# Householder tridiagonalization: sums over partitions in four column groups, and dot products formed by TensorE in the last 127 steps

## The chip, the cores and the metric

One NeuronCore of a Trainium2 chip runs the whole program. The metric is the device time in microseconds of one execution. TensorE is PE in the rows below (PEld its weight loads), VectorE DVE, ScalarE ACT, GpSimd POOL and SyncE SP.

## What is computed

The reference runs a graph network with LSTM windows on `x` (16 x 512 x 128) and `adj` (512 x 512), adds it to `x`, normalizes, then runs a spectral graph network and normalizes again. The spectral network needs all eigenvectors `U` of a symmetric 512 x 512 matrix:

```python
deg = jnp.sum(A, axis=0) + jnp.sum(A, axis=1) - jnp.diagonal(A)
d_inv_sqrt = jnp.where(deg > 0, jax.lax.rsqrt(deg), 0.0)
L_norm = d_inv_sqrt[:, None] * (jnp.diag(deg) - A) * d_inv_sqrt[None, :]
_, U = jnp.linalg.eigh(L_norm)
h = jax.nn.relu(jnp.einsum('mn,bnd->bmd', U.T, features) @ W1 + b1)
return jnp.einsum('nm,bmd->bnd', U, h @ W2 + b2)
```

The kernel finds them by reducing `L_norm` to tridiagonal form with Householder reflectors, solving that small problem, and turning the vectors back. Everything is float32. The change lies in the reduction.

## The kernel before

The matrix stands in SBUF as `lap`, 128 partitions x 4 tiles x 512 columns. The reduction is one loop of 510 steps (`STEPS`), written out in full on each engine; the engines meet through semaphores. Step k works on column k + 1 below the diagonal, in the tiles from `t0 = (k + 1) // 128` on, so on T = 4 - t0 tiles: T is 4 for the first 127 steps, 3 and 2 for 128 each, 1 for the last 127. Updates of the matrix are held back in a panel of 16 steps (`NB`, `j = k % 16`); the panel is the last 128 columns of `lapw`. Every 16th step PE applies it as a rank-32 product (L581 to L586), and DVE adds that to `lap` (L990).

In a step, with `a` the column (`acols[:, t0:, k]`), `v` the reflector, and `y`, `p`, `w` vectors of the same length:

- DVE's `norms` (L969, L970) puts the head of `a` (alpha) and each partition's share of a.a into `xn`. PE sums over the partitions with a matmul whose weights are all ones (L574); the total then stands in every partition of PSUM bank 0. ACT takes the root (L349), and DVE forms the reflector from it (L994 to L1004).
- PE forms the product of the matrix and panel with `a` (L591): the weights are the column `a`, repeated in 32 columns, and four column groups of the array each stream their own strips of 32 columns of each tile. For this loop there are 8 T matmuls in the trace, since each float32 matmul stands there as two.
- PE picks the row of the panel that the reflector starts in (L595, a 128-column weight `unit(k)`), and sums the squares of the tail (L599), which POOL has prepared (L307 to L320).
- DVE reduces the products to `ycol` and `a1` (L1007 to L1021), multiplies and reduces v.y to one number a partition (L1023), PE sums it (L601); the same for v.p (L1041, L603). The sum of v.y is needed for the next column (L1044), that of v.p for `w` (L1049, L1052).
- L1044 writes column k + 1 of `acols`; `norms(k + 1)` follows at once, then L1049 and L1052, then the next step's L994. L1052 releases the next step's L591.

All five partition sums and the panel row are a 128 x 128 weight and one or a few moving columns:

```python
pe.matmul(bank[0][:, 0:2], ones[:, 0:P], xn[:, 0:2], start=True, stop=True).then_inc(norm_ps, 1)
pe.matmul(bank[3][:, 0:1], ones[:, 0:P], xp[:, 0:1], start=True, stop=True).then_inc(vy_ps, 1)
```

The order of work on each engine is the order in which it stands in the code; nothing else schedules it. PE takes for step k: L574, L591, L595, L599, L601, L603. DVE's order is its list above; `put` and `after` are semaphores between DVE's own instructions. ACT takes in a step L349, L352 (copy of `w`), L358, L360 and L361 (copies of `v`), L363 (`w0`, p times tau) and L365. POOL takes L307 and one to four more for the tail.

Of the kernel before, what the change touches and what calls it, by code (L numbers as in the profile page):

```python
# [5 lines left out]
ALU = mybir.AluOpType  # L6
ACT = mybir.ActivationFunctionType
# [5 lines left out]
P = 128  # L13
N = 512
# [132 lines left out]
def program(nc, x, adj, wg0, bg0, wg1, bg1, wih, whh, bih, bhh, w1, b1, w2, b2, out):  # L147
    with ExitStack() as ctx:
        def sb(name, shape, dt=F32):
            return ctx.enter_context(nc.sbuf_tensor(name, shape, dt))  # L150

        def sem(name):
            return ctx.enter_context(nc.semaphore(name))
# [13 lines left out]
        a1 = sb("a1", [P, NT]); ycol = sb("ycol", [P, NT]); pcol = sb("pcol", [P, NT])  # L167
        bm = sb("bm", [P, NT]); ats = sb("ats", [P, NT]); w0 = sb("w0", [P, NT]); jcol = sb("jcol", [P, 3, NT]); xp = sb("xp", [P, 2]); ts = sb("ts", [P, 8])
        tail = sb("tail", [P, N])
# [65 lines left out]
        a_ready = sem("a_ready"); norm_in = sem("norm_in"); tail_link = sem("tail_link"); tail_in = sem("tail_in"); tail_ps = sem("tail_ps"); v2_ready = sem("v2_ready"); edge_ready = sem("edge_ready"); p_ready = sem("p_ready"); w0_ready = sem("w0_ready"); norm_ps = sem("norm_ps"); norm_root = sem("norm_root"); rowz_ps = sem("rowz_ps")  # L235
        y_done = sem("y_done"); x_ready = sem("x_ready"); vy_ps = sem("vy_ps"); vy_saved = sem("vy_saved"); x2_ready = sem("x2_ready"); vp_ps = sem("vp_ps")
        w_ready = sem("w_ready"); w2_ready = sem("w2_ready"); panx_ps = sem("panx_ps"); panx_sb = sem("panx_sb"); update_ps = sem("update_ps"); updated = sem("updated")
# [40 lines left out]
        def _(pool):  # L278
# [53 lines left out]
        def _(act):  # L332
# [204 lines left out]
        def _(pe):  # L537
# [29 lines left out]
            def unit(k):  # L567
                return ident[:, (k + 1) % P:(k + 1) % P + 1].to_broadcast([P, P])

            for k in range(STEPS):  # L570
                t0, j = (k + 1) // P, k % NB
                T, c0 = NT - t0, t0 * P
                pe.wait_ge(norm_in, 2 * (k + 1))
                pe.matmul(bank[0][:, 0:2], ones[:, 0:P], xn[:, 0:2], start=True, stop=True).then_inc(norm_ps, 1)  # L574
                if k:
# [23 lines left out]
                pe.matmul(bank[4][:, 0:1], ones[:, 0:P], xn[:, 2:3], start=True, stop=True).then_inc(tail_ps, 1)  # L599
                pe.wait_ge(x_ready, k + 1)  # L600
                pe.matmul(bank[3][:, 0:1], ones[:, 0:P], xp[:, 0:1], start=True, stop=True).then_inc(vy_ps, 1)  # L601
                pe.wait_ge(x2_ready, k + 1)
                pe.matmul(bank[2][:, 4 * NB:4 * NB + 1], ones[:, 0:P], xp[:, 1:2], start=True, stop=True).then_inc(vp_ps, 1)  # L603
# [269 lines left out]
        def _(dve):  # L873
# [108 lines left out]
            for k in range(STEPS):  # L982
                t0, j = (k + 1) // P, k % NB
                T, c0 = NT - t0, t0 * P
                v, a_ = vcols[:, t0:, k], acols[:, t0:, k]
                if j == 0 and k:
                    for t in range(t0, NT):
                        adds += 1
                        dve.wait_ge(update_ps, adds)
                        m = V.tensor_tensor(lap[:, t, first_live(k):], lap[:, t, first_live(k):], bank[4 + t][:, first_live(k):], ALU.add)  # L990
                    m.then_inc(updated, 1)

                dve.wait_ge(norm_root, k + 1)
                put(V.reciprocal(ts[:, 3:4], ts[:, 0:1]))  # L994
                a = put(V.tensor_scalar(ts[:, 1:2], bank[0][:, 1:2], 0.0, 0.5, ALU.is_ge, ALU.subtract))
# [4 lines left out]
                b = put(V.scalar_tensor_tensor(pair[:, k, 1:2], ts[:, 4:5], ts[:, 1:2], bank[0][:, 1:2], ALU.mult, ALU.add))  # L1000
                after(a)
# [14 lines left out]
                after(a)  # L1016
                y = put(V.tensor_reduce(ycol[:, t0:], yz[:, t0:, 0:32 + 2 * j], AX.X, ALU.add))  # L1017
# [11 lines left out]
                p = put(V.scalar_tensor_tensor(pcol[:, t0:], a1[:, t0:], pair[:, k, 0:1], ycol[:, t0:], ALU.mult, ALU.add))  # L1029
                after(g)  # L1030
# [9 lines left out]
                c = put(V.scalar_tensor_tensor(ats[:, t0:], a_, scrow[:, k:k + 1], ltm[:, t0:, k + 1], ALU.mult, ALU.mult))  # L1040
                V.tensor_tensor_reduce(jcol[:, 2, t0:], v, pcol[:, t0:], 0.5, 0.0, ALU.mult, ALU.add, xp[:, 1:2]).then_inc(x2_ready, 1)  # L1041
# [9 lines left out]
                dve.wait_ge(w0_ready, k + 1)  # L1051
                V.scalar_tensor_tensor(pan[:, t0:, :, j, 0], v.unsqueeze(2).to_broadcast([P, T, 4]), ts[:, 6:7], w0[:, t0:].unsqueeze(2).to_broadcast([P, T, 4]),  # L1052
# [911 lines left out]
```

## Time and profile before

| | |
|---|---|
| time, median of 3 runs | 5219.31 us (5218.76 to 5219.66) |
| time of the profiled execution | 5220.33 us |
| its span | 5218.5 us |
| DVE busy | 4171.1 us, 80% |
| PE busy | 3302.7 us, 63% |
| chain that ended last | DVE 61%, PE 30%, issue 6%, ACT 1% |
| reduction (first L994 to the last) | 56.4 to 2756.4 us |

The profile is one execution. The chain that ended last goes backwards from the end, at each step to what released the waiting instruction. A row's idle time is that of its engine just before it, with what ended it. Ends of matmuls are modelled. What follows the reduction is the LSTM network, the tridiagonal solver and the spectral network; the change leaves their instructions as they are.

### The profile page before, as it was taken

Reading aid. Unit: us, or ns where it says so; the run is one execution under the profiler, and the core shown is the slowest. Engines: PE = TensorE matmul, PEld = TensorE weight load, DVE = VectorE, ACT = ScalarE, POOL = GpSimd, SP = SyncE. Lnnn points to the kernel's source line nnn. Section 1 sums busy time; section 2 is a strip of 40 time slices with the busy share of each in tenths; the row PEclk is TensorE's granted clock in tenths of the full one; section 3 lists DMA queues with packets and bytes.
Section 4 is the critical chain, followed back from the end, with each engine's and each line's share of the span. In section 5 each row is a group of like instructions: output and inputs, shape, how many; then the busy total and the mean of one; then the engine's idle time right before and its main releaser. Section 6 shows DMA issues by size and latency. Waiting matters only on the chain.

```text
span 5218.5 us, 76031 instructions
## 1 busy us (share of the span) xinstructions
PE 3302.7 (63%) x18918; PEld 2330.4 (45%) x18918; DVE 4171.1 (80%) x26705; ACT 1070.2 (21%) x4761; POOL 362.2 (7%) x1807
## 2 busy tenths in 40 slices
PE   6888888878887777777776764656722232234148
PEld 4556665666666666666663221222212232223124
DVE  7666666777777888888888999999977888988956
ACT  1111111222222222222221123433301200200001
POOL 1111111111111111100000000000000000000000
PEclk5555555555555555555557777878955555656669
DMA  2000000000000000000000000000000000000001
GB/s 65 1 1 1 1 1 1 2 1 1 2 1 1 1 1 1 1 1 1 1 1 1 1 1 1 1 1 1 1 1 1 0 0 0 0 0 0 0 0 33
DMA packets 20810, 17.51 MB, mean 3 GB/s; under 512 B 6544, under 2 KB 16784, under 8 KB 20368
## 3 DMA queue, kind: packets, MB, share of 16 engines
q1 hardware_dynamic: 20368, 12.65, 0.9%
q8 instruction: 152, 2.49, 0.2%
q14 instruction: 290, 2.38, 0.2%
HBM read 8.41 MB, written 4.20 MB: 2 GB/s over the span
## 4 chain that ended last, share of the span: by engine, by line
DVE 61%; PE 30%; issue 6%; ACT 1%; SPq 0%; DMA 0%; POOL 0%; DVEq 0%
PE bank L591 10%; PE bank L603 6%; PE bank L595 3%; PE bank L574 3%; DVE qp L1384 2%; DVE ycol L1017 2%; DVE dif L1746 2%; PE bank L586 2%; DVE tau_row L1033 2%; DVE ts L1049 2%; DVE qp L1371 2%; DVE jcol L1041 2%; DVE gated L1031 1%; DVE lapw L1052 1%; DVE pcol L1029 1%
## 5 line engine op out<-in xcount | busy, mean ns | idle before, releaser
L591 PE MATMUL bank<-lapw,hid 128*32 128x160 f32 (+3 forms) x10200 | 660.4, 421 | 59.1 <-DVE lapw L990 16.2
L662 PE MATMUL bank<-hid,rows 128*128 128x512 f32 (+1 forms) x504 | 318.2, 797 | 275.8 <-ACT dif L397 273.6
L591 PEld LDWEIGHTS bank<-lapw,hid 128*32 128x32 f32 x10200 | 394.7, 162 | 184.2 <-DVE lapw L1052 82.2
L603 PE MATMUL bank<-xp,ones 128*128 128x1 f32 x1020 | 298.9, 362 | 278.6 <-DVE xp L1041 278.6
L601 PE MATMUL bank<-xp,ones 128*128 128x1 f32 x1020 | 298.9, 362 | 185.4 <-DVE xp L1023 185.4
L603 PEld LDWEIGHTS bank<-xp,ones 128*128 128x128 f32 x1020 | 255.3, 311 | 322.1 <-DVE xp L1041 322.1
L601 PEld LDWEIGHTS bank<-xp,ones 128*128 128x128 f32 x1020 | 255.3, 311 | 229.1 <-DVE xp L1023 229.1
L360 ACT ACTIVATE swap<-vcols 128x4 f32<-128x4 f32 (+3 forms) x510 | 105.5, 207 | 1148.6 <-DVE xp L1023 1148.6
L662 PEld LDWEIGHTS bank<-hid,rows 128*128 128x128 f32 x504 | 117.1, 239 | 468.4 <-ACT dif L397 299.6
L574 PE MATMUL bank<-xn,ones 128*128 128x2 f32 x1020 | 299.2, 363 | 18.6 <-DVE xn L970 17.3
L595 PEld LDWEIGHTS bank<-lapw,ident 128*128 128x128 f32 x956 | 240.2, 313 | 157.9 <-issue 157.9
L595 PE MATMUL bank<-lapw,ident 128*128 128x2 f32 (+1 forms) x956 | 291.9, 385 | 0.0
L599 PE MATMUL bank<-xn,ones 128*128 128x1 f32 x1020 | 289.1, 353 | 0.0
L599 PEld LDWEIGHTS bank<-xn,ones 128*128 128x128 f32 x1020 | 277.5, 332 | 10.6 <-issue 10.6
L1007 DVE TENSOR_TENSOR yz<-bank,pick 128x128 f32<-128x128 f32 (+3 forms) x510 | 117.8, 231 | 204.2 <-PE bank L591 204.0
L574 PEld LDWEIGHTS bank<-xn,ones 128*128 128x128 f32 x1020 | 255.3, 311 | 44.5 <-DVE xn L970 20.9
L307 POOL TENSOR_TENSOR sq<-hid,ltm 128x4 f32<-128x4 f32 (+3 forms) x510 | 101.0, 198 | 2302.3 <-DVE hid L1044 2250.6
L745 PE MATMUL bank<-wide,ones 128*128 128x128 f32 x80 | 18.3, 402 | 293.1 <-DVE wide L1502 293.1
L1049 DVE TENSOR_SCALAR ts<-bank,tau_row 128x1 f32<-128x1 f32 x510 | 141.4, 277 | 64.4 <-PE bank L603 1.1
L349 ACT ACTIVATE ts<-bank 128x1 f32<-128x1 f32 x510 | 87.2, 171 | 456.2 <-PE bank L574 456.2
L363 ACT ACTIVATE w<-pcol,tau_row 128x4 f32<-128x4 f32 (+3 forms) x510 | 150.9, 296 | 115.0 <-DVE tau_row L1033 115.0
L994 DVE RECIPROCAL ts<-ts 128x1 f32<-128x1 f32 x510 | 83.3, 163 | 101.1 <-ACT ts L349 100.8
(752 smaller groups left out, 7994.1 us busy)
## 6 DMA issues: line engine op xcount, KB each, us to landing
out_x<-xs SPq DMA_DIRECT2D x16, 256.0 KB, 3.0
lapw<-in_adj SPq DMA_DIRECT2D x1, 1024.0 KB, 5.6
bias_rows<-in_L_gnn_bg SPq DMA_DIRECT2D x8, 64.0 KB, 6.0
hid<-pair SPq DMA_DIRECT2D x32, 1.0 KB, 1.7
bias_rows<-in_L_gnn_b SPq DMA_DIRECT2D x4, 64.0 KB, 5.8
wg<-in_L_gnn_Wg SPq DMA_DIRECT2D x2, 64.0 KB, 4.9
wg<-in_L_gnn_W SPq DMA_DIRECT2D x2, 64.0 KB, 4.5
dif<-in_L_gnn_Wih SPq DMA_DIRECT2D x1, 0.5 KB, 6.4
```

What stands on the lines that cost most here:

```text
L360: act.activation(swap[:, t0:, j, 0], vcols[:, t0:, k], ACT.Copy)
L363: act.activation(w0[:, t0:], pcol[:, t0:], ACT.Copy, scale=tau_row[:, k:k + 1]).then_inc(w0_ready, 1)
L574: pe.matmul(bank[0][:, 0:2], ones[:, 0:P], xn[:, 0:2], start=True, stop=True).then_inc(norm_ps, 1)
L586: pe.matmul(bank[4 + t][:, first_live(k):], panx[:, 0, t * P:(t + 1) * P], panx[:, 1, first_live(k):], start=True, stop=True).then_inc(upd ...
L591: m = pe.matmul(bank[1][32 * q:32 * q + 32, 0:(T + 1) * 32].rearrange("p (u i) -> p u i", i=32), acols[:, t, k:k + 1].to_broadcast([P, 32] ...
L595: pe.matmul(bank[2][:, 0:2 * j], unit(k), lapw[:, t0, N:N + 2 * j], start=True, stop=True).then_inc(rowz_ps, 1)
L599: pe.matmul(bank[4][:, 0:1], ones[:, 0:P], xn[:, 2:3], start=True, stop=True).then_inc(tail_ps, 1)
L601: pe.matmul(bank[3][:, 0:1], ones[:, 0:P], xp[:, 0:1], start=True, stop=True).then_inc(vy_ps, 1)
L603: pe.matmul(bank[2][:, 4 * NB:4 * NB + 1], ones[:, 0:P], xp[:, 1:2], start=True, stop=True).then_inc(vp_ps, 1)
L662: m = pe.matmul(bank[4 * h + q][:, 0:cols_], wih_t[:, p - 1, q * P:(q + 1) * P], hid[:, b0:b0 + nb, t:t + (nw - 1) * p + 1:p], start=True, ...
L1007: a = put(V.tensor_tensor(yz[:, t0:, 0:32], bank[1][:, 0:T * 32].rearrange("p (t i) -> p t i", i=32), pick[:].unsqueeze(1).to_broadcast([P ...
L1049: a = put(V.tensor_scalar(ts[:, 6:7], bank[2][:, 4 * NB:4 * NB + 1], tau_row[:, k:k + 1], tau_row[:, k:k + 1], ALU.mult, ALU.mult))
```

## The change

Two things change. First, `everywhere` replaces each full-width sum and the panel row by four matmuls, one for each column group, with 32 weight columns each; every group writes its own 32 partitions of the same PSUM column. This holds in all 510 steps.

Second, in the steps with one tile left (`dots(k)`, k from 383 to 509) PE forms four dot products itself with `product`: one vector is the weight, repeated in 32 columns, the other the moving column. These are a.a (alpha comes from a sum of its own with `unit(k)`), the tail, v.y and v.p. `norms`, L1023 and L1041 fall away on DVE in these steps, and POOL's second product. The small constants that those instructions carried move: 1e-32 of a.a becomes a bias `tiny` of 1e-30 under ACT's root, and the factor 0.5 of v.p becomes a copy of tau times 0.5 on ACT (`ts[:, 7:8]`). DVE's wait for `w0_ready` stands one instruction earlier in all steps.

```diff
+DOT_TILES = 1
+def dots(k):
+    return NT - (k + 1) // P <= DOT_TILES
...
 (POOL)
                 if k:
                     pool.wait_ge(tail_ps, k)
+                if dots(k):
+                    pool.tensor_tensor(sq[:, 0, t0:], acols[:, t0:, k], ltm[:, t0:, k + 1], ALU.mult).then_inc(tail_in, 1)
+                    continue
...
 (ACT)
-                act.activation(ts[:, 0:1], bank[0][:, 0:1], ACT.Sqrt).then_inc(norm_root, 1)
+                if dots(k):
+                    act.activation(ts[:, 0:1], bank[0][:, 0:1], ACT.Sqrt, bias=tiny[:]).then_inc(norm_root, 1)
+                else:
+                    act.activation(ts[:, 0:1], bank[0][:, 0:1], ACT.Sqrt).then_inc(norm_root, 1)
...
                 act.wait_ge(p_ready, k + 1)
+                if dots(k):
+                    act.activation(ts[:, 7:8], tau_row[:, k:k + 1], ACT.Copy, scale=0.5)
...
 (PE)
             def unit(k):
-                return ident[:, (k + 1) % P:(k + 1) % P + 1].to_broadcast([P, P])
+                return ident[:, (k + 1) % P:(k + 1) % P + 1].to_broadcast([P, 32])
+            def everywhere(into, weights, column):
+                for q in range(4):
+                    m = pe.matmul(into[32 * q:32 * q + 32, :], weights, column, start=True, stop=True)
+                return m
+            def product(into, left, right):
+                for q in range(4):
+                    for t in range(T):
+                        m = pe.matmul(into[32 * q:32 * q + 32, :], left[:, t:t + 1].to_broadcast([P, 32]), right[:, t:t + 1], start=(t == 0), stop=(t == T - 1))
+                return m
...
-                pe.wait_ge(norm_in, 2 * (k + 1))
-                pe.matmul(bank[0][:, 0:2], ones[:, 0:P], xn[:, 0:2], start=True, stop=True).then_inc(norm_ps, 1)
+                if dots(k):
+                    pe.wait_ge(a_ready, k + 1)
+                    product(bank[0][:, 0:1], acols[:, t0:, k], acols[:, t0:, k]).then_inc(norm_ps, 1)
+                    everywhere(bank[5][:, 0:1], unit(k), acols[:, t0, k:k + 1]).then_inc(alpha_ps, 1)
+                else:
+                    pe.wait_ge(norm_in, 2 * (k + 1))
+                    everywhere(bank[0][:, 0:2], ones[:, 0:32], xn[:, 0:2]).then_inc(norm_ps, 1)
...
-                    pe.matmul(bank[2][:, 0:2 * j], unit(k), lapw[:, t0, N:N + 2 * j], start=True, stop=True).then_inc(rowz_ps, 1)
+                    everywhere(bank[2][:, 0:2 * j], unit(k), lapw[:, t0, N:N + 2 * j]).then_inc(rowz_ps, 1)
...
+                if dots(k):
+                    product(bank[4][:, 0:1], sq[:, 0, t0:], sq[:, 0, t0:]).then_inc(tail_ps, 1)
+                    pe.wait_ge(x_ready, k + 1)
+                    product(bank[3][:, 0:1], vcols[:, t0:, k], ycol[:, t0:]).then_inc(vy_ps, 1)
+                    pe.wait_ge(x2_ready, k + 1)
+                    product(bank[2][:, 4 * NB:4 * NB + 1], vcols[:, t0:, k], pcol[:, t0:]).then_inc(vp_ps, 1)
+                else:
+                    everywhere(bank[4][:, 0:1], ones[:, 0:32], xn[:, 2:3]).then_inc(tail_ps, 1)
...
 (DVE)
+                alpha = bank[5][:, 0:1] if dots(k) else bank[0][:, 1:2]
...
                 dve.wait_ge(norm_root, k + 1)
+                if dots(k):
+                    scalars += 1
+                    dve.wait_ge(alpha_ps, scalars)
...
+                if dots(k):
+                    V.tensor_reduce(ycol[:, t0:], yz[:, t0:, 0:32 + 2 * j], AX.X, ALU.add).then_inc(x_ready, 1)
...
-                after(max(y, vdone))
-                V.tensor_tensor_reduce(jcol[:, 1, t0:], v, ycol[:, t0:], 1.0, 0.0, ALU.mult, ALU.add, xp[:, 0:1]).then_inc(x_ready, 1)
+                if not dots(k):
+                    after(max(y, vdone))
+                    V.tensor_tensor_reduce(jcol[:, 1, t0:], v, ycol[:, t0:], 1.0, 0.0, ALU.mult, ALU.add, xp[:, 0:1]).then_inc(x_ready, 1)
...
-                if k + 1 < STEPS:
+                if k + 1 < STEPS and not dots(k + 1):
                     norms(k + 1)
                 dve.wait_ge(vp_ps, k + 1)
-                a = put(V.tensor_scalar(ts[:, 6:7], bank[2][:, 4 * NB:4 * NB + 1], tau_row[:, k:k + 1], tau_row[:, k:k + 1], ALU.mult, ALU.mult))
+                dve.wait_ge(w0_ready, k + 1)
+                half = ts[:, 7:8] if dots(k) else tau_row[:, k:k + 1]
+                a = put(V.tensor_scalar(ts[:, 6:7], bank[2][:, 4 * NB:4 * NB + 1], tau_row[:, k:k + 1], half, ALU.mult, ALU.mult))
```

L1029 (`pcol`) releases `x2_ready` in these steps, and L1041 is left out in the same way as L1023.

## Rows read from the trace of the kernel before

**Rows 1.** Busy time by stretch: T = 4, 3, 2 and 1; PEclk is the clock.

```profile
56.40:898.40 842.00, 694.24 (x5438) 505.21 (x5434) 546.68 (x3822) 155.39 (x904) 125.44 (x635) 0.50 0.01 1
898.40:1609.80 711.40, 572.56 (x4436) 454.72 (x4432) 527.63 (x3849) 154.67 (x914) 100.25 (x511) 0.50 0.01 1
1609.80:2207.40 597.60, 470.85 (x3384) 386.84 (x3380) 490.98 (x3841) 150.97 (x914) 74.92 (x383) 0.50 0.01 1
2207.40:2756.40 549.00, 396.99 (x2289) 333.39 (x2288) 455.63 (x3772) 145.35 (x900) 48.60 (x252) 0.50 0.00 1
```

**Rows 2.** DVE by line: T = 4 (two rows), 3, 2; after the bar idle us.

```profile
L1007 DVE TENSOR_TENSOR yz<-bank,pick 128x128 f32<-128x128 f32 x127 | 37.1, 292 | 155.7 <-PE bank L591 155.7
L1015 DVE TENSOR_TENSOR tz<-swap,bank 128x8 f32<-128x8 f32 (+14 forms) x119 | 26.3, 221 | 11.0
...
L1015 DVE TENSOR_TENSOR tz<-swap,bank 128x90 f32<-128x90 f32 (+14 forms) x120 | 24.6, 205 | 17.0 <-PE bank L595 6.0
...
L1015 DVE TENSOR_TENSOR tz<-swap,bank 128x60 f32<-128x60 f32 (+14 forms) x120 | 22.5, 188 | 2.8
```

**Rows 3.** Timeline of one step with T = 3: start, us, instruction, idle before.

```profile
1599.82 0.87 PE L591 MATMUL bank<-lapw,hid 128*32 128x128 f32 x12
...
1600.76 0.26 DVE L1007 TENSOR_TENSOR yz<-bank,pick 128x96 f32<-128x96 f32 x1 [0.37 <-PE bank L591]
1600.93 0.23 DVE L1012 TENSOR_TENSOR yz<-swap,bank 128x78 f32<-128x78 f32 x1
...
1601.44 0.33 DVE L1017 TENSOR_REDUCE ycol<-yz 128x3 f32<-128x174 f32 x1
...
1601.90 0.09 DVE L1023 DVE_READ_ACCUMULATOR2_ANT xp<- 128x1 f32 x1
1601.90 0.16 DVE L1025 TENSOR_SCALAR vrow<-bank 128x1 f32<-128x1 f32 x1
...
1603.17 0.58 PE L603 MATMUL bank<-xp,ones 128*128 128x1 f32 x2 [0.54 <-DVE xp L1041]
...
1603.60 0.08 DVE L970 DVE_READ_ACCUMULATOR2_ANT xn<- 128x1 f32 x1
...
1603.80 0.28 DVE L1049 TENSOR_SCALAR ts<-bank,tau_row 128x1 f32<-128x1 f32 x1
```

**Rows 4.** Timeline with T = 1: one step's end, then the next step's y and a1.

```profile
2602.88 0.22 DVE L1040 SCALAR_TENSOR_TENSOR ats<-hid,scrow,ltm 128x1 f32<-128x1 f32 x1
...
2603.14 0.23 DVE L1044 SCALAR_TENSOR_TENSOR hid<-ats,bank,bm 128x1 f32<-128x1 f32 x1
...
2604.40 0.17 ACT L349 ACTIVATE ts<-bank 128x1 f32<-128x1 f32 x1 [0.83 <-PE bank L574]
...
2604.45 0.44 PE L591 MATMUL bank<-lapw,hid 128*32 128x64 f32 x8
...
2604.60 0.16 DVE L994 RECIPROCAL ts<-ts 128x1 f32<-128x1 f32 x1 [0.20 <-ACT ts L349]
...
2605.98 0.17 DVE L1021 TENSOR_REDUCE a<-tz 128x1 f32<-128x21 f32 x1
...
2606.26 0.21 DVE L1029 SCALAR_TENSOR_TENSOR pcol<-a,pair,ycol 128x1 f32<-128x1 f32 x1
```

**Rows 5.** PE matmuls by form: ns min/median/max of one, first and last start.

```profile
L591 PE MATMUL bank<-lapw,hid x8: 314/315/316, 2604.5 to 2604.6; 128*32 128x64 f32 x8
...
L591 PE MATMUL bank<-lapw,hid x24: 421/421/423, 1604.4 to 1605.5; 128*32 128x128 f32 x24
...
L603 PE MATMUL bank<-xp,ones x1020: 352/362/373, 60.5 to 2759.5; 128*128 128x1 f32 x170
...
L595 PE MATMUL bank<-lapw,ident x18: 371/394/417, 1481.4 to 1523.0; 128*128 128x14 f32 x2, 128*128 128x16 f32 x2, 128*128 128x18 f32 x2, 128*128 128x20 f32 x2
```

**Rows 6.** ACT in one step with T = 3, from the timeline.

```profile
1602.56 0.30 ACT L363 ACTIVATE w<-pcol,tau_row 128x3 f32<-128x3 f32 x1 [0.21 <-DVE tau_row L1033]
...
1604.41 0.20 ACT L352 ACTIVATE swap<-lapw 128x3 f32<-128x3 f32 x1
```

More of the change, by code:

```diff
@@ L167, in program @@
         a1 = sb("a1", [P, NT]); ycol = sb("ycol", [P, NT]); pcol = sb("pcol", [P, NT])
-        bm = sb("bm", [P, NT]); ats = sb("ats", [P, NT]); w0 = sb("w0", [P, NT]); jcol = sb("jcol", [P, 3, NT]); xp = sb("xp", [P, 2]); ts = sb("ts", [P, 8])
+        bm = sb("bm", [P, NT]); ats = sb("ats", [P, NT]); w0 = sb("w0", [P, NT]); jcol = sb("jcol", [P, 3, NT]); xp = sb("xp", [P, 2]); tiny = sb("tiny", [P, 1]); ts = sb("ts", [P, 8])
         tail = sb("tail", [P, N])
@@ L235, in program @@
         a_ready = sem("a_ready"); norm_in = sem("norm_in"); tail_link = sem("tail_link"); tail_in = sem("tail_in"); tail_ps = sem("tail_ps"); v2_ready = sem("v2_ready"); edge_ready = sem("edge_ready"); p_ready = sem("p_ready"); w0_ready = sem("w0_ready"); norm_ps = sem("norm_ps"); norm_root = sem("norm_root"); rowz_ps = sem("rowz_ps")
-        y_done = sem("y_done"); x_ready = sem("x_ready"); vy_ps = sem("vy_ps"); vy_saved = sem("vy_saved"); x2_ready = sem("x2_ready"); vp_ps = sem("vp_ps")
+        y_done = sem("y_done"); alpha_ps = sem("alpha_ps"); x_ready = sem("x_ready"); vy_ps = sem("vy_ps"); vy_saved = sem("vy_saved"); x2_ready = sem("x2_ready"); vp_ps = sem("vp_ps")
         w_ready = sem("w_ready"); w2_ready = sem("w2_ready"); panx_ps = sem("panx_ps"); panx_sb = sem("panx_sb"); update_ps = sem("update_ps"); updated = sem("updated")
@@ L598, in _ @@
                 pe.wait_ge(tail_in, k + 1)
[L599 to L603, printed above, removed]
+                if dots(k):
[6 more added lines that the diff above has]
+                    everywhere(bank[4][:, 0:1], ones[:, 0:32], xn[:, 2:3]).then_inc(tail_ps, 1)
+                    pe.wait_ge(x_ready, k + 1)
+                    everywhere(bank[3][:, 0:1], ones[:, 0:32], xp[:, 0:1]).then_inc(vy_ps, 1)
+                    pe.wait_ge(x2_ready, k + 1)
+                    everywhere(bank[2][:, 4 * NB:4 * NB + 1], ones[:, 0:32], xp[:, 1:2]).then_inc(vp_ps, 1)
             j = STEPS % NB
@@ L606, in _ @@
             pe.wait_ge(v2_ready, STEPS)
-            pe.matmul(bank[2][:, 0:2 * j], unit(STEPS), lapw[:, NT - 1, N:N + 2 * j], start=True, stop=True).then_inc(rowz_ps, 1)
+            everywhere(bank[2][:, 0:2 * j], unit(STEPS), lapw[:, NT - 1, N:N + 2 * j]).then_inc(rowz_ps, 1)
             pe.wait_ge(diag_in, 1)
@@ L946, in _ @@
             V.memset(swap[:], 0.0)
+            V.memset(tiny[:], 1e-30)
             V.memset(pair[:], 0.0)
@@ L973, in _ @@
             adds = 0
-            rowz = 0
+            rowz = scalars = 0
             def panel_rows(row, j, T):
@@ L993, in _ @@
                 dve.wait_ge(norm_root, k + 1)
+                if dots(k):
+                    scalars += 1
+                    dve.wait_ge(alpha_ps, scalars)
                 put(V.reciprocal(ts[:, 3:4], ts[:, 0:1]))
-                a = put(V.tensor_scalar(ts[:, 1:2], bank[0][:, 1:2], 0.0, 0.5, ALU.is_ge, ALU.subtract))
+                a = put(V.tensor_scalar(ts[:, 1:2], alpha, 0.0, 0.5, ALU.is_ge, ALU.subtract))
                 after(a)
@@ L999, in _ @@
                 a = put(V.tensor_tensor(pair[:, k, 0:1], ts[:, 4:5], ts[:, 1:2], ALU.mult))
-                b = put(V.scalar_tensor_tensor(pair[:, k, 1:2], ts[:, 4:5], ts[:, 1:2], bank[0][:, 1:2], ALU.mult, ALU.add))
+                b = put(V.scalar_tensor_tensor(pair[:, k, 1:2], ts[:, 4:5], ts[:, 1:2], alpha, ALU.mult, ALU.add))
                 after(a)
@@ L1016, in _ @@
                 after(a)
-                y = put(V.tensor_reduce(ycol[:, t0:], yz[:, t0:, 0:32 + 2 * j], AX.X, ALU.add))
+                if dots(k):
+                    V.tensor_reduce(ycol[:, t0:], yz[:, t0:, 0:32 + 2 * j], AX.X, ALU.add).then_inc(x_ready, 1)
+                else:
+                    y = put(V.tensor_reduce(ycol[:, t0:], yz[:, t0:, 0:32 + 2 * j], AX.X, ALU.add))
                 if j:
@@ L1028, in _ @@
                     dve.wait_ge(w0_ready, k)
-                p = put(V.scalar_tensor_tensor(pcol[:, t0:], a1[:, t0:], pair[:, k, 0:1], ycol[:, t0:], ALU.mult, ALU.add))
+                p = V.scalar_tensor_tensor(pcol[:, t0:], a1[:, t0:], pair[:, k, 0:1], ycol[:, t0:], ALU.mult, ALU.add)
+                if dots(k):
+                    p.then_inc(x2_ready, 1)
+                else:
+                    put(p)
                 after(g)
@@ L1040, in _ @@
                 c = put(V.scalar_tensor_tensor(ats[:, t0:], a_, scrow[:, k:k + 1], ltm[:, t0:, k + 1], ALU.mult, ALU.mult))
-                V.tensor_tensor_reduce(jcol[:, 2, t0:], v, pcol[:, t0:], 0.5, 0.0, ALU.mult, ALU.add, xp[:, 1:2]).then_inc(x2_ready, 1)
+                if not dots(k):
+                    V.tensor_tensor_reduce(jcol[:, 2, t0:], v, pcol[:, t0:], 0.5, 0.0, ALU.mult, ALU.add, xp[:, 1:2]).then_inc(x2_ready, 1)
                 after(c)
```

1 line of the change is left out of this document (removed).

## The prediction

> **What bounds the kernel now.** I first read the page's chain of waits: it runs through DVE and PE and hardly through the transfers. The change touches the tridiagonalization alone, so I then read a table of its four stretches, cut where a tile of the matrix drops out [rows 1]. They take 842, 711, 598 and 549 us for 127, 128, 128 and 127 steps: means of 6.63, 5.56, 4.67 and 4.32 us a step. The granted clock is 0.50 in each, TensorE's lower level of 1.2 GHz, although PE counts as busy for 72 to 82% of them; it can't fall further, and I take it to stay.
>
> Next, DVE's idle time by line [rows 2], and one step each with three tiles and with one, in order of time [rows 3, 4]. DVE is one serial chain. Each step it waits for: the sum for vp before L1049; the square root before L994, which itself waits for the norm's sum (L574); with four and three tiles the matrix product, before L1007 (155.7 us over 127 steps with four); and the panel row (L595), before L1015. With one tile only the first two are left.
>
> **What a sum costs.** In [rows 3] L603 starts at 1603.17 and L1049, which waits for it, at 1603.80: 0.63 us. L574 is the same instruction pair. Each such sum is two matmuls (each float32 matmul stands as two in the trace) with 128 weight columns, 0.58 together.
>
> After the change it is eight with 32 weight columns. No row has such a sum, so I build it from the matrix product, which has this shape with more moving columns. One such matmul takes 315 ns at 64 columns and 421 at 128 [rows 5]: 1.66 ns a column, so 210 ns at one column. The eight at 64 columns take 0.44 in all [rows 4], 0.125 more than one alone. At one column the second wave of four waits only for its weights: two full-width matmuls lie 0.23 apart (0.58 less the 0.35 of one, [rows 5]), a quarter of the width makes 0.06, and the four of a wave add 0.02. So 0.29. The product's reader starts 0.07 after its end ([rows 3]: 1599.82 + 0.87, then 1600.76). Sum to reader: **0.37 us, against 0.63: 0.26 gained** (an estimate). The ends: 0.30 if the second wave costs nothing (gain 0.33), 0.51 if one column costs what 64 do (0.12), 0.63 if width buys nothing, and worse below. I take 0.37, since the rows show that duration falls with the column count.
>
> A rule speaks against this. The Trainium skill, TensorEngine Tiling (Array Packing), Instruction Overhead, says that a matmul with one moving column has the latency of one with about 60, and advises against tiling a dimension that is already small. By it a sum would cost the 64-column figure, 0.51; it is the second rival.
>
> **The change, part by part.**
>
> (a) *L1049 earlier.* In [rows 3] the last DVE work before it, L970's read-out, starts at 1603.60, and a short DVE instruction starts beside such a read-out (L1025 at 1601.90, as L1023's). L1049 starts at 1603.80, kept by L603. With 0.37 the sum is there at 1603.54, so DVE sets the start: 0.20 gained. With four tiles and three this brings L1052, the matrix product and L1007 forward by as much.
>
> (b) *L595 becomes eight small matmuls behind the product's.* Now L1015 waits for it: 0.14 us a step with three tiles (17.0 us over 120), 0.09 with four, 0.02 with two [rows 2]. The gain is larger, because without a wait DVE starts an instruction some 0.08 before the last one ends. In [rows 3] L1017 needs L1012's result, ready at 1601.16, so could start at 1601.22: it starts at 1601.44, 0.22 later. With the idle time of [rows 2] and the same 0.08 it is 0.17 to 0.18 with four tiles and some 0.09 with two.
>
> (c) *The norm's sum* shortens the way to the square root by 0.26. With two tiles this sets L994 and all after it. With more it is hidden under the product.
>
> (d) *The last 127 steps.* The partial sums on DVE go (L969, L970, L1023, L1041), POOL's second product too. PE starts a.a straight from L1044. Today L1044 to L994 is 2603.14 to 2604.60, 1.46 us [rows 4]. New: L1044's result reaches PE after 0.28 (0.23 for it, 0.05 of signal); a.a 0.37; the square root 0.17, and 0.10 more for its new bias operand, as L363 with its scale operand takes 0.30 beside 0.20 for L352 [rows 6]; 0.03 to DVE. That is 0.95: 0.51 gained. L1023's removal lets L1029 start when L1021's result is there (2605.98 + 0.17 + 0.03 = 2606.18, not 2606.26): 0.07. L1041's removal gains nothing, because L1044 waits for L1040 (2602.88 + 0.22 + 0.03) anyway. Together 0.58.
>
> What (d) adds: PE's seven products a step are 56 matmuls. The second sum (alpha) follows a.a by two waves, 0.15, while the square root takes 0.27: hidden. ACT's extra copy (0.17) and L363 end some 0.2 before L1049 can start. That start moves up by 0.6 and now waits for vp and w0, both earlier. v.y starts when y is there, 1.2 us ahead of its reader L1044. Cover for all of these is 0.1 to 1.2 us; with a price of 0.07 for every matmul the alpha sum would be late first.
>
> **The sum.** Steps into a rank-32 update (8 in each stretch) have the norm hidden, and gain (a) alone.
> - four tiles: 119 x (0.20 + 0.18) + 8 x 0.20 = 47
> - three: 120 x (0.20 + 0.22) + 8 x 0.20 = 52
> - two: 120 x (0.26 + 0.09) + 8 x 0.20 = 44
> - one: 127 x 0.58 = 74
>
> In all 217 us. The profiled execution took 5220.3 us (span 5218.5), 1.0 above the median of 5219.3. So 5220 less 217: **5003 us**. If waves cost nothing (gain 0.33), the 247 steps with two tiles and one give 17 more; if the bias operand is free, 13 more: 4973 at the low end.
>
> **The rivals.**
>
> *One column costs what 64 do* (0.51 a sum). (a) gives 0.12, the norm 0.12, the last stretch 0.44: 37 + 42 + 26 + 56 = 161, so 5059 us. For it: a floor per wave isn't visible where columns are many. Against it: the slope in [rows 5], and L603's one column takes 352 to 373 ns where L595's 14 to 20 take 371 to 417.
>
> *Four column groups buy no latency at all* (0.63). Then (a) and (c) give nothing; (b) stays, and (d) keeps 0.32: 21 + 26 + 11 + 41 = 99, so 5121 us. Against it: the 64-column product's 0.44 beside L603's 0.58.
>
> *Slower: PE takes its instructions one after another.* The place is the PE queue; the price is a fixed time for each of the eight, from the three-tile product, 12 in 0.87 [rows 3], 0.0725 each. Then a sum costs 7 x 0.0725 + 0.28 = 0.79. L1049 comes 0.16 late, the norm with two tiles 0.19 late, and alpha, 16 in line, makes L994 0.22 late in the last stretch, of which 0.07 is won back: +2, +7, -13, -19, 23 us lost, 5243 us. It decides from about 0.07 us a matmul. Against it: eight run in 0.44 [rows 4], where this would give 7 x 0.0725 + 0.315 = 0.82. The Trainium skill, TensorE: Matmul & The Clock Gate, Back-to-back issue gap, gives some 62 ns per MATMUL for the sequencer when hardware decode is off; by it a sum would be 0.71 and the time 5189 us. The 0.44 speaks against this too.
>
> *The last stretch's path isn't shortened*, because another wait (alpha, w0, y) takes the root's place: 217 less 74 leaves 143, 5077 us.
>
> **How the numbers follow.** 0.63 for the forecast, 0.14 for the 64-column price, 0.07 for no latency gain, 0.06 for the last stretch alone failing, 0.06 for slower, 0.04 for anything else, half faster, half the same. The range: from 4973 up to 5080, which takes in the second rival and the last one. A measurement here can tell about 0.2%, 10 us. Faster by over 0.2%: 0.92; within 0.2%: 0.02; slower: 0.06.
>
> **What would show it.** A sum of eight matmuls with 0.29 to 0.30 us from first start to last end, its reader 0.37 after the start; L1049's and L1015's waits gone; steps of 6.25, 5.15, 4.33 and 3.74 us; in the last stretch L994 0.95 after L1044, waiting for the root. Wrong, if small matmuls in a wave start more than 0.02 apart, if L1049 still waits for PE, or if L994 waits for the alpha sum.

## The result and the profile after

The changed kernel takes 5015.8 us (median of 4 runs, 5013.2 to 5016.7) against 5219.3 us before: a ratio of 0.9609, 95% interval 0.9593 to 0.9626. Forecast were 5003 us. The profiled execution has a span of 5011.4 us, 207 less than before.

Lines have moved: L622 is now the matrix product (L591 before), L586 all sums and the panel row, L593 the dot products, L1037 is L994, L1050 L1007, L1055 L1012, L1058 L1015, L1063 L1017, L1096 L1044, L1103 L1049 and L1105 L1052.

Busy time of the four stretches of the changed kernel, cut at the same steps and with the same columns as [rows 1]:

```profile
55.00:858.60 803.60, 486.96 (x9195) 339.04 (x9188) 533.99 (x3823) 166.84 (x904) 125.61 (x636) 0.50 0.01 2
858.60:1525.80 667.20, 364.39 (x8228) 287.05 (x8229) 515.31 (x3849) 165.68 (x913) 99.98 (x512) 0.50 0.01 2
1525.80:2079.40 553.60, 263.43 (x7176) 210.14 (x7176) 480.20 (x3838) 162.14 (x912) 74.70 (x382) 0.50 0.01 2
2079.40:2551.00 471.60, 207.82 (x7036) 159.62 (x7040) 399.85 (x2892) 168.76 (x1026) 24.12 (x126) 0.50 0.01 3
```

Each row begins with the window and its length; behind them stands PE's busy time with its count.

| tiles | before | after | saved | forecast |
|---|---|---|---|---|
| 4 | 842.0 | 803.6 | 38 | 47 |
| 3 | 711.4 | 667.2 | 44 | 52 |
| 2 | 597.6 | 553.6 | 44 | 44 |
| 1 | 549.0 | 471.6 | 77 | 74 |

The sum is 204; what lies around the loop gives the other 3. PE executes twice as many matmuls in the loop (31,635 against 15,547) and is busy for less of it. The clock stays at 0.50.

DVE's groups in the stretches with four tiles (first three lines) and three, as [rows 2]:

```profile
L1050 DVE TENSOR_TENSOR yz<-bank,pick 128x128 f32<-128x128 f32 x127 | 37.0, 292 | 170.2 <-PE bank L622 170.2
L1103 DVE TENSOR_SCALAR ts<-bank,tau_row 128x1 f32<-128x1 f32 x127 | 35.2, 277 | 0.0
L1058 DVE TENSOR_TENSOR tz<-swap,bank 128x8 f32<-128x8 f32 (+14 forms) x119 | 25.4, 213 | 0.0
...
L1058 DVE TENSOR_TENSOR tz<-swap,bank 128x90 f32<-128x90 f32 (+14 forms) x120 | 23.7, 197 | 0.0
```

The waits for the sum (L1103; L1049 had 14.4 us with four tiles) and for the panel row (L1058: 11.0 and 17.0 us before) are gone. The wait for the matrix product has grown from 155.7 to 170.2 us: the root, and so DVE, is ready earlier behind the start of a product that takes as long as before.

One step with three tiles, to be held against [rows 3]:

```profile
1425.16 0.21 DVE L1055 TENSOR_TENSOR yz<-swap,bank 128x66 f32<-128x66 f32 x1
1425.29 0.21 DVE L1058 TENSOR_TENSOR tz<-swap,bank 128x66 f32<-128x66 f32 x1
1425.42 0.31 DVE L1063 TENSOR_REDUCE ycol<-yz 128x3 f32<-128x162 f32 x1
...
1426.51 0.30 ACT L376 ACTIVATE w<-pcol,tau_row 128x3 f32<-128x3 f32 x1 [0.21 <-DVE tau_row L1084]
...
1427.12 0.29 PE L586 MATMUL bank<-xp,ones 128*32 128x1 f32 x8 [0.84 <-DVE xp L1093]
...
1427.55 0.08 DVE L1009 DVE_READ_ACCUMULATOR2_ANT xn<- 128x1 f32 x1
1427.59 0.28 DVE L1103 TENSOR_SCALAR ts<-bank,tau_row 128x1 f32<-128x1 f32 x1
...
1427.68 0.29 PE L586 MATMUL bank<-xn,ones 128*32 128x2 f32 x8 [0.26 <-DVE xn L1009]
...
1428.03 0.17 ACT L360 ACTIVATE ts<-bank 128x1 f32<-128x1 f32 x1 [0.57 <-PE bank L586]
```

A sum takes 0.29 us as forecast, and its reader starts 0.35 after the sum's start (1427.68 to 1428.03; forecast 0.37, before 0.63). L1063 now starts 0.26 after L1055 (0.51 before). But L1103 starts 0.04 after the read-out before it and not with it. L376, which makes w0, had ended 0.78 us before L1103.

One step with one tile, to be held against [rows 4]:

```profile
2338.05 0.20 ACT L375 ACTIVATE ts<-tau_row 128x1 f32<-128x1 f32 x1 [0.35 <-DVE tau_row L1084]
...
2338.16 0.28 ACT L376 ACTIVATE w<-pcol,tau_row 128x1 f32<-128x1 f32 x1
...
2338.56 0.22 DVE L1096 SCALAR_TENSOR_TENSOR hid<-ats,bank,bm 128x1 f32<-128x1 f32 x1
2338.70 0.27 DVE L1103 TENSOR_SCALAR ts<-bank,tau_row,ts 128x1 f32<-128x1 f32 x1
...
2338.84 0.29 PE L593 MATMUL bank<-hid 128*32 128x1 f32 x8 [0.82 <-DVE hid L1096]
...
2338.97 0.27 PE L586 MATMUL bank<-hid,ident 128*32 128x1 f32 x8
...
2339.19 0.26 ACT L358 ACTIVATE ts<-bank,tiny 128x1 f32<-128x1 f32 x1 [0.21 <-PE bank L593]
...
2339.49 0.16 DVE L1037 RECIPROCAL ts<-ts 128x1 f32<-128x1 f32 x1 [0.25 <-ACT ts L358]
```

L1096 to L1037 is 0.93 us (1.46 before, 0.95 forecast). a.a is on PE 0.28 after L1096's start, the root follows 0.35 later and takes 0.26 with its bias. The alpha sum ends at 2339.24, 0.25 before L1037 starts: hidden. L376 ends 0.26 before L1103.

### The profile page after: what moved, and what is told of

Same layout as the page of the kernel before. It is cut to its first block, busy times and chain, and to the rows that moved or that the text cites. A ratio compares the mean times of both kernels' runs of the same rounds, so it can differ in the third digit from the quotient of the medians.

```text
span 5011.4 us, 107402 instructions
## 1 busy us (share of the span) xinstructions
PE 2489.1 (50%) x35048; PEld 1642.1 (33%) x35048; DVE 4079.0 (81%) x25817; ACT 1127.5 (22%) x4888; POOL 337.2 (7%) x1680
## 4 chain that ended last, share of the span: by engine, by line
DVE 69%; PE 21%; issue 8%; ACT 2%; SPq 0%; DVEq 0%; DMA 0%; POOL 0%
PE bank L622 10%; DVE qp L1437 2%; DVE dif L1799 2%; DVE hid L1096 2%; PE bank L617 2%; DVE tau_row L1084 2%; DVE qp L1424 2%; DVE gated L1082 2%; DVE pcol L1076 1%; DVE ts L1040 1%; DVE xn L1008 1%; DVE yz L1055 1%; DVE hid L1085 1%; PE bank L783 1%; DVE hid L1795 1%
## 5 line engine op out<-in xcount | busy, mean ns | idle before, releaser
L622 PE MATMUL bank<-lapw,hid 128*32 128x160 f32 (+3 forms) x10200 | 659.8, 420 | 109.7 <-DVE lapw L1105 86.7
L586 PE MATMUL bank<-xp,ones 128*32 128x1 f32 x6128 | 219.5, 202 | 672.0 <-DVE xp L1070 346.4
L622 PEld LDWEIGHTS bank<-lapw,hid 128*32 128x32 f32 x10200 | 393.9, 162 | 236.3 <-DVE lapw L1105 118.0
L586 PEld LDWEIGHTS bank<-xp,ones 128*32 128x32 f32 x6128 | 154.2, 140 | 737.1 <-DVE xp L1070 379.0
L1050 DVE TENSOR_TENSOR yz<-bank,pick 128x128 f32<-128x128 f32 (+3 forms) x510 | 117.8, 231 | 233.4 <-PE bank L622 233.2
L586 PE MATMUL bank<-xn,ones 128*32 128x2 f32 x6128 | 211.9, 198 | 118.1 <-DVE xn L1009 118.1
L586 PEld LDWEIGHTS bank<-xn,ones 128*32 128x32 f32 x6128 | 169.1, 149 | 152.4 <-DVE xn L1009 151.0
L586 PEld LDWEIGHTS bank<-lapw,ident 128*32 128x32 f32 x3832 | 173.0, 176 | 22.1 <-DVE lapw L1105 1.3
L376 ACT ACTIVATE w<-pcol,tau_row 128x4 f32<-128x4 f32 (+3 forms) x510 | 148.9, 292 | 85.5 <-DVE tau_row L1084 85.5
L1040 DVE TENSOR_SCALAR ts<-ts,bank 128x1 f32<-128x1 f32 x510 | 141.1, 277 | 18.5
L586 PE MATMUL bank<-lapw,ident 128*32 128x2 f32 (+1 forms) x3832 | 147.4, 225 | 1.3 <-DVE lapw L1105 1.3
L1105 DVE SCALAR_TENSOR_TENSOR lapw<-vcols,ts,w 128x16 f32<-128x16 f32 (+3 forms) x510 | 120.4, 236 | 18.7
L1037 DVE RECIPROCAL ts<-ts 128x1 f32<-128x1 f32 x510 | 83.2, 163 | 61.8 <-ACT ts L358 29.2
L1437 DVE SCALAR_TENSOR_TENSOR qp<-qa,qn 32x1 f32<-32x1 f32 x540 | 111.6, 207 | 19.1
L369 ACT ACTIVATE tz<-lapw 128x4 f32<-128x4 f32 (+3 forms) x510 | 98.1, 192 | 111.8 <-DVE lapw L1030 111.8
```

What stands on the lines that cost most here:

```text
L586: m = pe.matmul(into[32 * q:32 * q + 32, :], weights, column, start=True, stop=True)
L622: m = pe.matmul(bank[1][32 * q:32 * q + 32, 0:(T + 1) * 32].rearrange("p (u i) -> p u i", i=32), acols[:, t, k:k + 1].to_broadcast([P, 32] ...
L1050: a = put(V.tensor_tensor(yz[:, t0:, 0:32], bank[1][:, 0:T * 32].rearrange("p (t i) -> p t i", i=32), pick[:].unsqueeze(1).to_broadcast([P ...
L1437: a = mark(V.scalar_tensor_tensor(p_, qa[:, 20 + i:21 + i], qa[:, 20 + i:21 + i], qn[:, 1:2], ALU.mult, ALU.mult))
```

## The experiments

All run beside the kernel before; its medians there were 5219.3 to 5220.3 us. Where a time is compared with the changed kernel, it is with its median of 5015.8. Medians over steps are taken from the traces, over the steps of a stretch that are not next to a rank-32 update (with four tiles from step 34 on).

**The two halves, each alone.** `e1_sums_only` keeps the column groups and has no dot products:

```diff
-DOT_TILES = 1
+DOT_TILES = 0
```

> The column groups alone: no step has dot products on TensorE. Theory (each sum costs its reader 0.26 us less; the dot products are a separate gain in the last stretch): the first three stretches stay as in the changed kernel (804, 667 and 554 us), the last one gets the norm's 0.26 a step and nothing more, 3.93 us a step against 3.60 with the dot products, so 43 us more: 5059 us. Rival (the last stretch gained from the narrower sums alone, the dot products hide behind DVE): 5016 us, unchanged.

It took 5057.0 us, 41 more than the changed kernel; by the profiles the last stretch took 516.6 us, 45 more, and its median step 3.93 us. The rival is out: the dot products bring over 40 us on top of the narrow sums.

`e2_dots_only` keeps the dot products and gives every sum and the panel row of the other steps back their 128 weight columns (`everywhere` with a fourth operand is one full-width matmul):

```diff
+                if len(whole):
+                    return pe.matmul(into, whole[0], column, start=True, stop=True)
...
-                    everywhere(bank[0][:, 0:2], ones[:, 0:32], xn[:, 0:2]).then_inc(norm_ps, 1)
+                    everywhere(bank[0][:, 0:2], ones[:, 0:32], xn[:, 0:2], ones[:, 0:P]).then_inc(norm_ps, 1)
...
```

> The dot products alone: the last 127 steps as in the changed kernel, the sums and the panel row of the other 383 steps full-width again. Theory: the first three stretches return to the old 842, 711 and 598 us (127 us more), the last stays at 472: 5142 us. Rival (part of the gain in the first stretches came from the earlier wait for w0 or from elsewhere, not from the sums): clearly under 5142 us.

It took 5139.9 us; the stretches were 843, 712, 598 and 472 us. So all of the gain in the first three is the narrow matmuls'; the wait for w0, which is moved here too, brings none of it.

**The panel row.** `e3_row_full` gives only the panel row (L595 before) its full width again, in the first 383 steps:

```diff
-                    everywhere(bank[2][:, 0:2 * j], unit(k), lapw[:, t0, N:N + 2 * j]).then_inc(rowz_ps, 1)
+                    everywhere(bank[2][:, 0:2 * j], unit(k), lapw[:, t0, N:N + 2 * j], *([] if dots(k) else [unit(k, P)])).then_inc(rowz_ps, 1)
```

> Only the panel row of the first 383 steps has 128 weight columns again, all sums stay narrow. Theory (term b: y comes 0.17 earlier after the product with four tiles, 0.22 with three and 0.08 with two, because the row no longer waits for the array to empty): 20 + 26 + 10 = 56 us more, 5072 us. Rival (DVE's wait for the row is only its idle time, 0.09, 0.14 and 0.02 a step): 30 us more, 5046 us.

5079.6 us, 64 more. By stretch, with the columns of the first table:

```profile
55.60:879.00 823.40, 557.75 (x8479) 363.64 (x8474) 543.16 (x3824) 166.94 (x904) 124.53 (x636) 0.50 0.01 2
879.00:1571.10 692.10, 435.76 (x7508) 311.65 (x7512) 524.15 (x3850) 165.71 (x913) 99.15 (x512) 0.50 0.01 2
1571.10:2147.90 576.80, 334.64 (x6456) 243.49 (x6456) 488.00 (x3839) 162.12 (x912) 74.06 (x382) 0.50 0.01 2
```

That is 20, 25 and 23 us more: as the theory had it with four tiles and three (20, 26), but 23 instead of 10 with two. There I had taken the row's wait from the kernel before, in which DVE came to L1007, just ahead of the row, 0.11 us later behind L1052, which releases the product (medians over steps: 1.41 before, 1.30 here); with the root earlier the wide row is waited for. The row's instruction in the two-tile stretch of this run, to be held against the 2.8 us of [rows 2]:

```profile
L1060 DVE TENSOR_TENSOR tz<-swap,bank 128x60 f32<-128x60 f32 (+14 forms) x120 | 22.6, 188 | 15.8 <-PE bank L586 1.1
```

Its 0.13 us a step and the 0.08 by which DVE's instructions overlap make 0.21, or 25 us. The two gains depend on each other: the earlier root could not have been had in full without the narrow row.

**The wait for w0.** `e4_w0_back`:

```diff
                 dve.wait_ge(vp_ps, k + 1)
-                dve.wait_ge(w0_ready, k + 1)
+                if dots(k):
+                    dve.wait_ge(w0_ready, k + 1)
...
                 after(a)
+                if not dots(k):
+                    dve.wait_ge(w0_ready, k + 1)
```

> DVE's wait for w0 stands behind the first instruction for w again in the first 383 steps. In the changed kernel that instruction starts 0.042 us after the read-out before it, where 0 was forecast. Theory A (the second wait ahead of it costs 0.04 us of issue): 0.04 us a step with four and three tiles, 10 us in all, 5006 us. Theory B (DVE itself takes that long to follow on the read-out): no change, 5016 us.

4999.6 us (4999.6 to 5004.4). In the timeline of one three-tile step (its L1104 is the changed kernel's L1103):

```profile
1450.58 0.08 DVE L1009 DVE_READ_ACCUMULATOR2_ANT xn<- 128x1 f32 x1
1450.58 0.27 DVE L1104 TENSOR_SCALAR ts<-bank,tau_row 128x1 f32<-128x1 f32 x1
```

It starts with the read-out, as forecast for the change. The first two stretches are 800.2 and 661.8 us, 9 less together, and so is the profiled span (5002.6 against 5011.4). The medians lie 16 apart, because this run's profiled execution was its slowest (5004.4 us) and the changed kernel's its fastest (5013.2); between these two lie the same 9. Theory A holds for this place: with one more wait ahead of it the instruction starts 0.04 us later (medians over steps behind L1096: 0.57 and 0.53), although that wait had long been met.

**A sum's price by its columns.** `e5_wide64` streams 64 moving columns in each sum of the first 383 steps; the same values are repeated and only the first is read:

```diff
-                    everywhere(bank[3][:, 0:1], ones[:, 0:32], xp[:, 0:1]).then_inc(vy_ps, 1)
+                    everywhere(bank[3][:, 0:64], ones[:, 0:32], xp[:, 0:1].to_broadcast([P, 64])).then_inc(vy_ps, 1)
...
```

> The price of a sum by its columns: every sum of the first 383 steps streams 64 moving columns (the same one or two values repeated), and only the first is read; all else as in the changed kernel. Theory (1.66 ns a column at the end, and the second wave 0.107 instead of 0.055 behind the first): 0.16 us more a sum, from first start to reader 0.51 instead of 0.352. The sum for w then ends 0.06 after DVE's own bound with four and three tiles, the norm 0.16 later with two: 15 + 19 = 34 us more, 5050 us. Rival (a matmul with one column takes as long as one with 60 anyway): no change, 5016 us.

5028.9 us, 13 more. Timeline of one three-tile step, then the windows of the stretches with four, three and two tiles:

```profile
1447.78 0.44 PE L586 MATMUL bank<-xp,ones 128*32 128x64 f32 x8 [0.69 <-DVE xp L1093]
...
1448.21 0.08 DVE L1009 DVE_READ_ACCUMULATOR2_ANT xn<- 128x1 f32 x1
1448.30 0.28 DVE L1103 TENSOR_SCALAR ts<-bank,tau_row 128x1 f32<-128x1 f32 x1
```

```profile
56.00:843.20 787.20, 524.35 (x9192) 323.91 (x9188) 537.19 (x3823) 158.49 (x904) 124.43 (x636) 0.62 0.01 2
843.20:1516.80 673.60, 443.76 (x8228) 287.50 (x8228) 519.92 (x3848) 154.61 (x914) 99.11 (x511) 0.50 0.01 2
1516.80:2089.80 573.00, 342.35 (x7176) 210.13 (x7176) 484.14 (x3838) 151.32 (x912) 74.05 (x382) 0.50 0.01 2
```

The sum takes 0.44 instead of 0.29, so one column does not cost what 64 do. With three tiles and two the time grows by 6 and 19 us, as the theory had it (7.5 and 19). With four tiles it falls by 16 us, which neither theory expected: the granted clock there is 0.62, so TensorE ran part of that stretch at its upper level, and that shortened the matrix product for which DVE waits (449 ns for one of its matmuls on the mean, 474 in the changed kernel). The total is therefore no test of the price; the two stretches at 0.50 are.

**The root's bias.** `e8_no_bias` leaves out the 1e-30 under the root:

```diff
-act.activation(ts[:, 0:1], bank[0][:, 0:1], ACT.Sqrt, bias=tiny[:]).then_inc(norm_root, 1)
+act.activation(ts[:, 0:1], bank[0][:, 0:1], ACT.Sqrt).then_inc(norm_root, 1)
```

> The root in the last 127 steps without its bias operand (the 1e-30 under the root is left out). Theory (a pointer operand costs ACT 0.09 to 0.10 us, on the path to the next step): 0.09 x 119 = 11 us less, 5005 us. Rival (L994 waits for the alpha sum as soon as the root is earlier): less than half of that.

5005.3 us, 10.5 less (the last stretch 461.1 us, also 10.5 less), with

```profile
2332.15 0.17 ACT L358 ACTIVATE ts<-bank 128x1 f32<-128x1 f32 x1 [0.20 <-PE bank L593]
2332.35 0.16 DVE L1037 RECIPROCAL ts<-ts 128x1 f32<-128x1 f32 x1 [0.16 <-ACT ts L358]
```

0.17 instead of 0.26, all of it on the path.

**Dot products in more steps.** `e6_dots2` and `e6_dots4` raise `DOT_TILES`; a product's loop runs over tiles outside and column groups inside. `e6_dots4` begins at step 32, because the update at step 16 writes the column of bank 5 in which alpha stands:

```diff
-DOT_TILES = 1
+DOT_TILES = 4
-    return NT - (k + 1) // P <= DOT_TILES
+    return k >= 32 and NT - (k + 1) // P <= DOT_TILES
...
-                for q in range(4):
-                    for t in range(T):
+                for t in range(T):
+                    for q in range(4):
```

> Dot products on TensorE in the last 255 steps, two tiles and one (a product's loop goes over tiles first, then column groups). Theory: with two tiles the way from the new column to the root is 0.28 + 0.35 + 0.11 for two more waves + 0.32 = 1.06 against 1.20, and 0.07 from the removed share of v.y: 0.21 a step, 27 us less, 4989 us. Rival (the four further waves and alpha keep the matrix product from starting, so it becomes late): no gain or a loss in that stretch, 5016 us or more.

4984.4 us; the two-tile stretch 524.0 us, 30 less than 553.6 (forecast 27).

> Dot products on TensorE from step 32 on, so with four and three tiles too. There DVE's next step waits for the matrix product, which waits for w; w no longer stands behind the two instructions of the norm, 0.42 a step earlier, and 0.07 from the removed share of v.y, less 0.08 with four tiles, as a.a and alpha hold PE for 10 waves of 0.054. Theory: stretch one 39, two 62, three 27 us shorter: 4888 us. Rival (the products over several tiles make TensorE late): the first two stretches stay at 804 and 667 us or grow.

4889.6 us, a ratio of 0.9365 to the kernel before (0.9350 to 0.9381). Its first two stretches, and one four-tile step:

```profile
55.60:825.90 770.30, 589.13 (x19104) 461.47 (x19100) 495.92 (x3154) 175.74 (x999) 50.72 (x253) 0.50 0.02 4
825.90:1432.70 606.80, 454.37 (x17440) 398.07 (x17436) 463.50 (x2952) 177.97 (x1042) 25.11 (x128) 0.50 0.02 4
```

```profile
705.54 0.23 DVE L1096 SCALAR_TENSOR_TENSOR hid<-ats,bank,bm 128x4 f32<-128x4 f32 x1
...
705.83 0.61 PE L593 MATMUL bank<-hid 128*32 128x1 f32 x32 [0.44 <-DVE hid L1096]
...
706.00 0.25 DVE L1105 SCALAR_TENSOR_TENSOR lapw<-vcols,ts,w 128x16 f32<-128x16 f32 x1
...
706.27 0.27 PE L586 MATMUL bank<-hid,ident 128*32 128x1 f32 x8
...
706.38 2.34 PE L622 MATMUL bank<-lapw,hid 128*32 128x160 f32 x32
```

33, 60 and 30 us less in the three stretches (forecast 39, 62, 27). L1105 has w ready at 706.25; the product starts at 706.38, behind the last start of alpha's sum, and not 0.05 after w as in the changed kernel (medians over steps: 0.14 with four tiles, 0.05 with three).

**The best version, and a try at the clock.** `b1_best` starts at step 17 and moves the wait for w0 off the path:

```diff
+                if dots(k):
+                    dve.wait_ge(w0_ready, k + 1)
                 dve.wait_ge(vy_ps, k + 1)
...
                 dve.wait_ge(vp_ps, k + 1)
-                dve.wait_ge(w0_ready, k + 1)
...
+                if not dots(k):
+                    dve.wait_ge(w0_ready, k + 1)
```

> Dot products on TensorE from step 17 on, with the wait for w0 off DVE's way to w: ahead of the next column's instruction in these steps, behind the first instruction for w in the others. Theory: 15 more steps at 0.35 (5 us), and 0.04 a step with three tiles (5 us), none with four, where a.a and alpha hold TensorE until w is there: 4880 us. Rival (w0 is not there yet when the new column is due, and delays it): 4890 us or more.

4887.7 us (ratio 0.9362, 0.9348 to 0.9376), no more than 2 us below `e6_dots4`: the first stretch gives 4 us, the second none (607.2). One three-tile step of `e6_dots4`, with the wait for w0 ahead of L1103, and one of `b1_best`, with it ahead of L1098:

```profile
1201.23 0.23 DVE L1096 SCALAR_TENSOR_TENSOR hid<-ats,bank,bm 128x3 f32<-128x3 f32 x1
1201.38 0.27 DVE L1103 TENSOR_SCALAR ts<-bank,tau_row,ts 128x1 f32<-128x1 f32 x1
```

```profile
1201.17 0.23 DVE L1098 SCALAR_TENSOR_TENSOR hid<-ats,bank,bm 128x3 f32<-128x3 f32 x1
1201.31 0.27 DVE L1104 TENSOR_SCALAR ts<-bank,tau_row,ts 128x1 f32<-128x1 f32 x1
...
1201.62 0.24 DVE L1108 SCALAR_TENSOR_TENSOR lapw<-vcols,ts,w 128x12 f32<-128x12 f32 x1
...
1201.79 0.27 PE L586 MATMUL bank<-hid,ident 128*32 128x1 f32 x8
1201.92 1.51 PE L622 MATMUL bank<-lapw,hid 128*32 128x128 f32 x24
```

The first instruction for w starts 0.14 us behind the new column in both (medians over steps 0.143 and 0.144), and the new column itself starts 1.96 us behind L1050 in both. So here the wait had cost nothing, and w comes no sooner. The 0.04 of `e4_w0_back` belongs to the place behind the read-out.

`f96_fill` and `f192_fill` add useless columns behind v.p, to raise the clock on purpose:

```diff
+                    everywhere(bank[6][:, 0:FILL], ones[:, 0:32], ones[:, 0:FILL])
```

> As b1_best, and in each step with dot products TensorE streams 4 x 96 columns of ones into an unused bank behind v.p, in the time in which it would wait for the next column. Theory (TensorE's lower clock holds because it streams too little; widened sums had raised it to 0.61 in the first stretch): the clock rises above 0.61 in the first stretch and the matrix product there takes less of its 2.4 us, so clearly under 4880 us. Rival (no rise, or the filler is in the way of a.a): 4880 us or more.

> The same with 4 x 192 columns. Theory: a granted clock near 1.0 in the first stretches; the product with four tiles then takes about half of 2.4 us, and the steps with four tiles fall to the root's bound of some 4.3 us, with three to some 4.0: 4700 us. Rival (the filler's 0.64 us at the lower clock ends after the new column is there, and no rise): 0.1 to 0.2 us a step more, 4900 to 4950 us.

4898.7 and 4901.2 us, 11 and 13 more than `b1_best`. With 192 columns the first stretch reads

```profile
55.80:826.90 771.10, 642.33 (x21544) 491.98 (x21540) 490.29 (x3049) 176.77 (x1013) 38.63 (x193) 0.58 0.02 4
```

PE also stands still in products where the profile shows nothing that it waits for. These rows, from 56 to 900 us, are of `b1_best`, `f96_fill` and `f192_fill` in this order (line, us in total, times, longest; L594 is L593):

```profile
PE bank L593 <- issue: 1.2, 4, 0.3
PE bank L594 <- issue: 8.4, 17, 1.0
PE bank L594 <- issue: 9.2, 21, 0.9
```

The clock rises to 0.58 and not to 1.0, and the stretch is 5 us longer than without filler; with 96 columns it is 776.4 us at 0.52, 10 longer. The first theory fell. The new stalls are of the size of the loss. They sit in products and the profile shows no semaphore behind them; they are about as many with 96 columns as with 192, so they don't follow the columns. The supply of instructions is a candidate that wasn't tested, and `b1_best`, with 20,664 matmuls in its first stretch against 21,544, has only a few. The rival's other half, a filler that ends behind the new column, shows as well: up to 900 us PE waits for that column 125 times without filler and 28 times with 192 columns, but the root comes only 0.01 us later behind it (medians over steps with four tiles).

## Why the prediction was right, and where it was off

The forecast of 5003 us missed by 13, or 0.3%; the mechanism and the bounding waits are as described, and none of the rivals occurred.

- *The price of a sum* was the unknown. 0.29 us for eight matmuls and 0.37 to the reader were forecast, 0.29 and 0.35 came. The extrapolation from 64 and 128 columns to one held, and `e5_wide64` shows the same slope in the other direction. The Trainium skill, TensorEngine Tiling (Array Packing), Instruction Overhead, gives a matmul with one moving column the latency of one with 60. That does not hold here: eight matmuls with 64 columns took 0.44, with one column 0.29.
- *The slower rival* would have needed 0.07 us a matmul. In `e6_dots4` 32 matmuls take 0.61 us; less 0.20 for one alone, that leaves 0.013 from start to start. The Trainium skill, TensorE: Matmul & The Clock Gate, Back-to-back issue gap, gives some 62 ns per MATMUL for the case that hardware decode is off; nothing of that size shows here. In the sums of this rival the eight update steps are missing with four and three tiles: with them it is 25 us lost and 5245 us, and 5191 instead of 5189 for a sum of 0.71.
- *Term (a)* was mis-sized: 0.20 a step with four and three tiles, of which 0.16 came. What was wrong in it is "DVE sets the start" with the read-out: the moved wait for w0 stood in the diff, and (a) gave it no price. `e4_w0_back` puts that at 0.04 a step where it shows, 9 us in all, half of the 17 by which these two stretches fell short.
- *Term (b)* came as forecast with four and three tiles (0.17, 0.21 by `e3_row_full`). With two, L1007 to L1044 became 0.08 us shorter, as forecast (0.09; 2.8/120 and 0.08 make 0.10). But taking the narrow row away alone costs 23 us there and not 11 (120 x 0.09), because (c) depends on it.
- *Term (c)*, the root's sum, came as forecast: 0.28 shorter for 0.26.
- *Term (d)*: 0.61 for 0.58. L1044 to the root gave 0.53 of it, as a.a reached the root 0.02 sooner than forecast. The bias cost 0.09 of the 0.10 forecast (`e8_no_bias`). Of the stretch's 77 us the dot products bring 45 (471.6 against 516.6 in `e1_sums_only`) and the narrower sums 32.
- With four tiles the change brought 38 us for 47. By the traces, L1044 to L1049 is 0.148 shorter on the mean of all steps and L1007 to L1044 0.154: 19 us each, for 25 and 21. `e4_w0_back` gives 3 us back; the rest is open.

## What to carry to other kernels

A sum over partitions that one engine waits for is better made of four groups of 32 weight columns than of one of 128: the same numbers stand in every partition, here 0.28 us earlier. Where the operands are single columns, TensorE can form the dot product too. What that saves is the partial product and its signals on the serial engine, 0.35 us a step with one tile and with four, 0.47 with three and 0.23 with two; the change had left out all but the first. A gain that was sized from the waits of the old kernel can grow or shrink when another wait on the same path goes: the panel row with two tiles was worth twice its old wait. And a wait that has long been met need not be free: it cost 0.04 us behind DVE's read-out, and nothing behind the new column.

## What was not expected of the hardware

- TensorE's granted clock was 0.62 in the four-tile stretch of `e5_wide64`, whose sums stream 64 columns, and 0.58 with `f192_fill`, against 0.50 in the changed kernel and in `b1_best`. With three tiles it was 0.50 and 0.51 in the same two runs. In the kernel before PE counted as busy for 82% of the four-tile stretch, at 0.50; in `e5_wide64` it did for 67%, at 0.62. So the busier of the two had the lower clock.
- A second semaphore wait ahead of a DVE instruction, met for 0.78 us in the step shown, moved that instruction by 0.04 us behind a read-out and not at all in the steps with dot products.
- PE's `issue` waits in products: 17 and 21 of up to 1.0 us with the fillers, 4 of up to 0.3 in `b1_best`, 7 of up to 0.5 in `e6_dots4`, none in the changed kernel, from 56 to 900 us in each.
